# Attention and feed-forward block on one core: GpSimd takes four row scalings and one rope chunk of the opening, whose order of work is rewritten

## The reference

```python
y = x * rsqrt(mean(x * x) + 1e-6) * rms_w
q, k, v = split(einsum('bsm,cm->bsc', y, w_in))
q, k = rope(q), rope(k)
attn = softmax(where(causal, q @ k.T * 64 ** -0.5, -inf))
x1 = layernorm(x + (x + (attn @ v) @ w_out.T))
out = layernorm(x1 + (x1 + ternary(x1) @ (ternary(weight) + rram).T))
```

## Time and profile before

| | us |
|---|---|
| median of 3 runs | 1446.98 |
| lowest and highest | 1443.99, 1448.08 |
| the profiled execution | 1443.82 |
| its span | 1442.0 |

### The profile page before, as it was taken

How to read it: one execution, slowest core, us unless ns; L and a number is a source line. 1 busy time by engine, 2 the same in 40 slices (tenths; PEclk the granted TensorE clock), 3 DMA queues, 4 the chain that set the end, 5 groups by cost and what they waited for, 6 DMA issues and landing times.

```text
span 1442.0 us, 24292 instructions
## 1 busy us (share of the span) xinstructions
PE 1355.3 (94%) x7296; PEld 1106.9 (77%) x7296; DVE 1117.4 (77%) x2519; ACT 1082.9 (75%) x2277; POOL 873.2 (61%) x846
## 2 busy tenths in 40 slices
PE   4789999999999999999999999999999999996896
PEld 3677787878878787888878787888878788785674
DVE  4677877877786878778787887778787787776997
ACT  4777778787787788778787878778787878775563
POOL 1456566475646656476646657376646667477866
PEclk9899999999999999999999999999999999999999
DMA  6001110111101111111101111111101111011011
GB/s 204 23 25 48 44 34 27 55 27 44 38 16 52 51 32 31 52 30 41 39 18 52 49 34 30 45 38 41 35 22 52 49 32 31 26 36 56 23 63 66
DMA packets 45154, 61.74 MB, mean 43 GB/s; under 512 B 10464, under 2 KB 27104, under 8 KB 45024
## 3 DMA queue, kind: packets, MB, share of 16 engines
q1 hardware_dynamic: 45024, 60.20, 14.2%
HBM read 34.74 MB, written 4.46 MB: 27 GB/s over the span
## 4 chain that ended last, share of the span: by engine, by line
PE 70%; DVE 12%; issue 6%; ACT 6%; DMA 2%; POOL 2%; SPq 1%; DVEq 0%; POOLq 0%; ACTq 0%
PE x L1078 17%; PE s L1066 15%; PE t L1112 13%; PE x L1096 9%; PE ot L1032 7%; PE ot L1030 7%; DVE prob_lo L997 3%; DVE prob L929 3%; ACT prob L766 2%; DMA spread<-recip_rows 1%; ACT prob_hi L737 1%; DVE stats L828 1%; PE x L1086 1%; ACT q_t L801 1%; DVE acc L990 1%
## 5 line engine op out<-in xcount | busy, mean ns | idle before, releaser
L997 DVE TENSOR_TENSOR prob_lo<-t,prob_hi 128x512 fp32r<-128x512 f32 x576 | 393.9, 686 | 95.5 <-ACT prob_hi L737 90.8
L737 ACT ACTIVATE prob_hi<-t 128x512 fp32r<-128x512 f32 x576 | 341.7, 594 | 167.6 <-PE t L1112 161.6
L929 DVE CUSTOM_DVE_ANT_0 prob<-s,mask 128x896 f32<-128x896 f32 (+7 forms) x512 | 382.0, 752 | 76.0 <-PE s L1066 63.0
L1066 PE MATMUL s<-k_t,q_t 128*128 128x512 f32 (+3 forms) x1536 | 385.1, 365 | 31.1 <-DVE neg_max L929 25.3
L766 ACT ACTIVATE prob<-prob,neg_max 128x896 f32<-128x896 f32 (+7 forms) x512 | 393.2, 769 | 22.3 <-DVE neg_max L929 20.1
L1112 PE MATMUL t<-ident,prob 128*128 128x128 f32 x2304 | 346.2, 273 | 2.0 <-ACT prob L766 2.0
L1112 PEld LDWEIGHTS t<-ident,prob 128*128 128x128 f32 x2304 | 286.4, 140 | 79.0 <-ACT prob L766 5.5
L1066 PEld LDWEIGHTS s<-k_t,q_t 128*128 128x128 f32 x1536 | 257.2, 191 | 87.4 <-DVE neg_max L929 46.0
L1030 PE MATMUL ot<-prob_hi,v_sb 128*128 128x512 f32 x576 | 242.9, 422 | 0.0
L1032 PE MATMUL ot<-prob_lo,v_sb 128*128 128x512 f32 x576 | 231.7, 402 | 11.2 <-DVE prob_lo L997 10.9
L710 POOL TENSOR_TENSOR o_lo<-o_raw,o_hi 128x256 fp32r<-128x256 f32 x128 | 94.6, 739 | 217.2 <-ACT o_hi L821 216.3
(11 more groups left out here) (86 smaller groups left out, 1949.9 us busy)
## 6 DMA issues: line engine op xcount, KB each, us to landing
swapped<-flat SPq DMA_DIRECT2D x320, 64.0 KB, 2.0
spread<-recip_rows SPq DMA_DIRECT2D x128, 128.0 KB
recip_rows<-turned SPq DMA_DIRECT2D x512, 0.5 KB
raw<-L_attn_w_in SPq DMA_DIRECT2D x8, 768.0 KB, 4.5
raw<-L_attn_w_out SPq DMA_DIRECT2D x8, 512.0 KB, 3.6
out<-acc SPq DMA_DIRECT2D x16, 256.0 KB, 2.0
acc<-L_attn_x SPq DMA_DIRECT2D x3, 1024.0 KB, 10.0
acc<-L_attn_x SPq DMA_DIRECT2D x4, 256.0 KB, 3.7
```

The costliest lines, as they stand in the source:

```text
L737: act.activation(prob_hi[:, u % 2, :], t_ps[u % 2][:, :], ACT.Copy).then_inc(prob_hi_done, 1)
L929: dve.tensor_tensor_reduce(out=prob_row(s, h), in0=s_ps[:, off:off + cols], in1=mask[:, KEYS - cols:KEYS], scale=-DH ** -0.5, scalar=3e38, ...
L997: dve.tensor_tensor(prob_lo[:, u % 2, :], t_ps[u % 2][:, :], prob_hi[:, u % 2, :].bitcast(F32), ALU.subtract).then_inc(prob_lo_done, 1)
L1066: mm = pe.matmul(s_ps[:, off + c * P:off + c * P + cols], q_t[:, h, s * P:(s + 1) * P], k_t[:, part, keys:keys + cols], start=(part == 0), ...
```

## The change

Three things are edited. The list `FIRST` is replaced by another order of the same entries. POOL does `xn` of tiles 4 to 7 (`POOL_NORMS`) instead of DVE. POOL does `ro` and `hl` of chunk 1 (`POOL_CHUNK`) in the first stage instead of DVE, with the code that it has for the passes. Chunks 2 and 0 stay on DVE. The waits that go with it: POOL's scaling of tile t waits for `rstd`, for the scaling before it and for the scratch tile to be free (`y_lo_done` at t − 2); DVE's scaling of tile 8 waits for POOL's of tile 7; POOL's rope in the first stage waits for the tables, for the stored chunk and for the rope before it, and its split for the split before it.

```diff
+POOL_CHUNK = 1
+POOL_NORMS = (4, 5, 6, 7)
 FIRST = (
-    ('sq', 0), ('xn', 0), ('xn', 1), ('xn', 2), ('norm', 0), ('xn', 3), ('norm', 1), ('w', 0), ('w', 1),
-    ('norm', 2), ('w', 2), ('norm', 3), ('w', 3), ('pj', 2, 0, 2), ('consts',), ('sw', 2, 0, 2), ('sq', 1),
-    ('pj', 2, 0, 0), ('ro', 2, 0, 2), ('xn', 4), ('hl', 2, 0, 2), ('pj', 2, 0, 1), ('sw', 2, 0, 0), ('vt', 2, 0),
-    ('ro', 2, 0, 0), ('sw', 2, 0, 1), ('xn', 5), ('norm', 4), ('hl', 2, 0, 0), ('ro', 2, 0, 1), ('sc', 2, 0, 0),
-    ('sc', 2, 0, 1), ('hl', 2, 0, 1), ('norm', 5), ('sc', 2, 0, 2), ('sc', 2, 0, 3), ('xn', 6), ('sc', 2, 1, 0),
-    ('ex', 2, 0, 0), ('sc', 2, 1, 1), ('ex', 2, 0, 1), ('ex', 2, 0, 2), ('sc', 2, 1, 2), ('ex', 2, 0, 3),
-    ('ex', 2, 1, 0), ('ex', 2, 1, 1), ('sc', 2, 1, 3), ('xn', 7), ('ex', 2, 1, 2), ('ex', 2, 1, 3), ('rc', 2, 0),
-    ('rc', 2, 1), ('norm', 6), ('norm', 7), ('rs', 2, 0), ('rs', 2, 1)
+    ('sq', 0), ('xn', 0), ('xn', 1), ('xn', 2), ('norm', 0), ('norm', 1), ('w', 0), ('xn', 3), ('w', 1), ('w', 2),
+    ('norm', 2), ('w', 3), ('norm', 3), ('pj', 2, 0, 2), ('sw', 2, 0, 2), ('ro', 2, 0, 2), ('sq', 1),
+    ('pj', 2, 0, 0), ('hl', 2, 0, 2), ('pj', 2, 0, 1), ('sw', 2, 0, 0), ('vt', 2, 0), ('ro', 2, 0, 0), ('xn', 4),
+    ('xn', 5), ('xn', 6), ('consts',), ('norm', 4), ('norm', 5), ('hl', 2, 0, 0), ('sc', 2, 0, 0),
+    ('sw', 2, 0, 1), ('xn', 7), ('sc', 2, 0, 1), ('norm', 6), ('norm', 7), ('sc', 2, 0, 2), ('sc', 2, 0, 3),
+    ('ex', 2, 0, 0), ('sc', 2, 1, 0), ('ex', 2, 0, 1), ('sc', 2, 1, 1), ('sc', 2, 1, 2), ('ro', 2, 0, 1),
+    ('rc', 2, 0), ('hl', 2, 0, 1), ('ex', 2, 0, 2), ('sc', 2, 1, 3), ('ex', 2, 0, 3), ('ex', 2, 1, 0),
+    ('rc', 2, 1), ('ex', 2, 1, 1), ('ex', 2, 1, 2), ('rs', 2, 0), ('ex', 2, 1, 3), ('rs', 2, 1)
 )
...
-                                or plan is first and e[0] in ("ro", "hl")):
+                                or plan is first and e[0] in ("ro", "hl") and e[3] != POOL_CHUNK
+                                or e[0] == "xn" and e[1] not in POOL_NORMS):
                             continue
+                        if e[0] == "xn":
+                            t = e[1]
+                            pool.wait_ge(rstd_done, t // 4 + 1)
+                            pool.wait_ge(xn_done, t)
+                            pool.wait_ge(y_lo_done, t - 2)
+                            pool.tensor_scalar(xn_tile(t), acc[:, t, :], rstd[:, t:t + 1], None, ALU.mult
+                                               ).then_inc(xn_done, 1)
...
+                            if plan is first:
+                                pool.wait_ge(table_in[half], 32)
+                                wait(pool, flat_done, g, CHUNKS, n + 1)
+                                wait(pool, roped, g, CHUNKS, n)
...
+                            if plan is first:
+                                wait(pool, parts_done, g, CHUNKS, n)
...
-                        elif e[0] == "ro" and plan is first:
+                        elif e[0] == "ro" and plan is first and e[3] != POOL_CHUNK:
...
-                        elif e[0] == "hl" and plan is first:
+                        elif e[0] == "hl" and plan is first and e[3] != POOL_CHUNK:
...
-                        elif e[0] == "xn":
+                        elif e[0] == "xn" and e[1] not in POOL_NORMS:
                             t = e[1]
                             dve.wait_ge(rstd_done, t // 4 + 1)
+                            if t - 1 in POOL_NORMS:
+                                dve.wait_ge(xn_done, t)
```

More of the change, by code:

```diff
@@ L614, in pool_idle @@
                     pool.wait_ge(rstd_done, what[0] + 1)
+                elif kind == "xn":
+                    pool.wait_ge(xn_done, what[0] + 1)
                 elif kind == "fl":
@@ L626, in one @@
                     for e in plan.ahead[u] + plan.behind[u]:
-                        if (e[0] not in ("ln", "res", "sq", "ro", "hl", "on", "oh", "fl", "x1")
-                                or plan is first and e[0] in ("ro", "hl")):
+                        if (e[0] not in ("ln", "res", "sq", "xn", "ro", "hl", "on", "oh", "fl", "x1")
+                                or plan is first and e[0] in ("ro", "hl") and e[3] != POOL_CHUNK
+                                or e[0] == "xn" and e[1] not in POOL_NORMS):
                             continue
+                        if e[0] == "xn":
[5 more added lines that the diff above has]
+                                               ).then_inc(xn_done, 1)
                         if e[0] == "fl":
```

## The result

The changed kernel takes 1449.80 us, the median of 19 runs (1447.56 to 1453.85), against 1447.84 of 19 runs of the kernel before on the same chips. The ratio is 1.0019, 95% interval 1.0010 to 1.0028: slower by 2.7 us (1.4 to 4.1); the two medians themselves differ by 2.0. The forecast was +6.7, with a range of +1.0 to +12.0 and the rival (a), no holding between VectorE and GpSimd, at +3.4.

What follows compares the result with a forecast made beforehand. TensorE, busy 94% of the span, was taken as the bound, so only its waits in the head count: head 2 9.0 later less 2.3 gives +6.7 us, 1453.7 against the median 1446.98; range 1448 to 1459.

Steps and rivals of the forecast that it cites:

- rival (a): Head, rope and split: VectorE and POOL do not hold each other; sum +3.4 us, 1450.4; chance 0.23.
- The direction and the path in the head: Head: slower; PE scores head 2 at 49.3 instead of 40.30, behind ScalarE's split and POOL's subtractions, 9.0 us later.
- What comes back: Between scores and opening: transposes of tiles 6 and 7 fall out, being done in the wait; 2.3 us back.
- The start's 0.25: Start of the head: tile 3's scaling no longer fills VectorE's wait for tile 1, so the first projection starts 0.25 later.
- What POOL's work does to VectorE's: Head: a VectorE operation with both inputs in SBUF waits for POOL's running one and ends 0.55 us later.
- The price of the scaling: Head, tiles 4 to 7: a scaling on POOL takes 1.55 us, ends 0.48 and 1.93.
- Its condition in the prediction: Head: the no-holding case decides once the holding between VectorE and POOL costs under 0.9 us in all.
- the first score: Head, PE's first score: forecast at 40.05 us, or 36.8 if rope and split are not held.
- the steps from there to head 2: Head, first score to head 2: scores, transposes, copies, exponentials, ScalarE's split, POOL's subtractions; from 40.05 to 49.3.
- one row: Row at 113.69: VectorE's scaling beside POOL took 1.41 instead of 0.48, ending 0.28 after POOL's; cited against no holding.
- the unheld sum: Whole kernel: the sum if rope and split are not held by POOL's work, +3.4 us.
- the relief: Head: 5.4 us of work off VectorE; as a rival, it shortens the head, about 1444; chance 0.08 with unseen reasons.

Runs made afterwards that it cites:

- e1_norms: Changed kernel with the old order of FIRST and only the scalings of tiles 4 to 7 on POOL; ratio 0.9999 to the kernel before, −0.1 us.
- e12_new_order_chunk: Changed kernel with the four scalings back on VectorE, third chunk on POOL, new order; ratio 1.0036 to the kernel before, +5.2 us.
- e6_two_inputs: Changed kernel with POOL's four scalings written as two-input operations; ratio 1.0042 to the kernel before, +6.1 us.
- e2_chunk: Kernel before, in its old order, with only the third chunk's rope and split on POOL; ratio 1.0019, +2.7 us.
- e3: Changed kernel with everything back on VectorE, third chunk's rope and split earlier in the new order; ratio 1.0020 to the kernel before, +2.9 us.
- e4: The list of e3 with the scalings of tiles 4 to 7 on POOL, third chunk on VectorE; ratio 0.9995 to the kernel before, −0.7 us.
- e7_hybrid: Scalings on POOL, third chunk on VectorE, transposes of tiles 5 to 7 ahead of head 2's score; ratio 0.9997 to the kernel before, −0.4 us.

## Why the prediction was wrong

**The direction and the path in the head were right.** Head 2 waits for POOL's last subtraction, ScalarE gets to the split only behind two copies and two exponentials, the transposes of tiles 6 and 7 fall out of the later stretch, the rest of the first pass keeps the shift. What comes back was forecast at 2.3 and is 2.1 (head 2 5.04 later, projection 2.94, both behind the first store, with the clock rising as the projection begins in both). The start's 0.25 is 0.3.

**The step that failed** is "What POOL's work does to VectorE's": that a VectorE operation with both inputs in SBUF waits for POOL's running one to its end. I took it from rows in which POOL's operation has two inputs and used it for scalings with one. Of the 6.7 us it carried 3.3, and in the measured time it carries at most 0.75. Measured, the scalings of 1.58 hold the K split not at all, the second rope by 0.4, the cast by 0.3 and the query split by 0.1; POOL is lengthened instead, which is hidden. e1_norms shows this by itself. Where POOL's operation has two inputs as well, the step is right even in its size: in e12_new_order_chunk VectorE's operations end 0.54 and 0.56 after POOL's, forecast 0.55, and e6_two_inputs brings the holding back by the second input. The price of the scaling, for which no row stood, was right: 1.55 forecast, 1.58 measured. Rival (a) was the case that came: +3.4 against +2.7, and it had a chance of 0.23. Its condition in the prediction, holding worth under 0.9 in all, is what the rows show. Head 2 itself came 5.13 later in the span where (a) had 5.75. Of the 0.6 between them half is there at the first score (36.52, forecast 36.8): tiles 4 and 5 were transposed in 1.38, ahead of the clock's fall at about 32 us, where I took twice 1.07. The other half is in the steps from there to head 2, 8.91 for 9.25.

**The weighing.** Against (a) I had one row, and for it the fact that POOL's operation there had two inputs and the scaling one. A row of another form should have widened the forecast to the unheld sum rather than carry its centre.

**What the relief was worth.** The four scalings off VectorE bought nothing in the old order (e1_norms −0.1), and the five operations of the third chunk off it cost 2.7 (e2_chunk). Those five and ScalarE's split between them are one chain, and on POOL each step is about 1.26 instead of 0.69: 2.9 us for five. From the rope's start to head 2 e2_chunk takes 8.16 where the kernel before takes 4.81, and the relief gives back only 0.45, by which the rope starts earlier. In the new order, with all on VectorE, the total is +2.9 (e3), with POOL's scalings −0.7 (e4): that order needs tiles 4 and 5 scaled beside VectorE's rope. This is the part of the change that does no harm; that it gains is not shown.

## What to carry to other kernels

Before moving a step to a slower engine, ask whether it lies on the chain that the bounding engine waits for; if it does, its longer duration is paid once for every step, however idle the slower engine is, and what it frees elsewhere is only worth the wait it ends. Move instead work that a later step needs and that can run beside the chain, as the scalings here, and order the list for it. When operations of two engines lengthen each other, take the price of their meeting from a row with the same number of inputs on both sides. And when a profile is read for where a gain went, compare the clock's rise and fall in both executions first.

## What the runs showed of the hardware

A one-input operation of GpSimd over 128x512 took 1.58 us. A two-input operation of VectorE issued 1.07 us after its start took its usual 0.68 (28.58 in the changed kernel, 28.36 in e1_norms); one issued 0.64 after the start of another took 1.06; and where VectorE was at work as GpSimd's began, GpSimd's took 2.03 to 2.10. With two inputs on GpSimd's side VectorE's took 1.05 to 1.64 for 0.69 (e6_two_inputs, e12_new_order_chunk). The Trainium skill, "SBUF — State Buffer", section "Who interferes with whom", gives the shared pair of ports to whoever issues first, for the whole instruction, and has the other fully block. With two inputs on both sides the trace agrees (ends 0.54 and 0.56 after GpSimd's). The row at 28.58 speaks against it for a one-input operation, where a reading part that is over early would fit (this was inferred, not measured by itself). The same scaling on GpSimd took twice what "GPSIMD Engine Reference" of the Trainium skill, "Elementwise — side-by-side cycle accounting", gives as the best case for 512 elements (769 ns); written with two inputs it took 1.04 (e6_two_inputs). And the clock moves places in a profile by as much as these changes do: its rise came from 44 to 56 us, and in four profiled executions (e1_norms, e3_order_dve, e6_two_inputs, e7_hybrid) it fell to its lower level again in the first pass, after PE had been idle for half of the time or more, and the stretch from the second to the third chunk's store was 1.2 to 2.1 us longer than before.
